# A decoder block on one core: head outputs turned in two fp32r parts, and the down products spread out between the turns

## The reference

```python
x = x + attn(layernorm(x))              # q, k, v; scores through a banded factor; softmax
x = x + xattn(layernorm(x), ctx, ctx)   # 8 heads of 32, exponential gates
x = x + ffn(layernorm(x))               # 256 -> 1024 -> 256, GELU, low-rank terms from the tokens
```

```python
maxit  = max(abs(sum(C, -1)), exp(-max_d))
H      = einsum('ij,jd->id', C, v) / (maxit + 1e-6)
xn     = (H - mean(H, over the 32 of the head)) / sqrt(var(H) + 1e-5)
out    = xn * gn_w + gn_b
```

## Time and profile before

| | |
|---|---|
| median of 3 runs | 1803.0 us |
| the profiled execution | 1803.04 us |
| its span from first to last instruction | 1801.3 us |
| mean granted TensorE clock, share of full | 0.984 |
| TensorE, products | 1742.0 us busy, 97% |
| TensorE, weight loads | 1376.2 us, 76% |
| VectorE | 1420.7 us, 79% |
| ScalarE | 1172.1 us, 65% |
| GpSimd | 402.0 us, 22% |
| mean DMA rate | 52 GB/s |

### The profile page before, as it was taken

How to read it: one execution, slowest core, us unless ns; L and a number is a source line. 1 busy time by engine, 2 the same in 40 slices (tenths; PEclk the granted TensorE clock), 3 DMA queues, 4 the chain that set the end, 5 groups by cost and what they waited for, 6 DMA issues and landing times.

```text
span 1801.3 us, 47658 instructions
## 1 busy us (share of the span) xinstructions
PE 1742.0 (97%) x15708; PEld 1376.2 (76%) x15708; DVE 1420.7 (79%) x4092; ACT 1172.1 (65%) x2666; POOL 402.0 (22%) x330
## 2 busy tenths in 40 slices
PE   5689999999999999999999999999999999999897
PEld 5568777777877777787777887777778777878676
DVE  6777888887888888788788888888888888887752
ACT  2556767666677766676766667776666676666552
POOL 1222122222122222212222212222221222222120
PEclk9789999999999999999999999999999999999998
DMA  5122121222112122212122211212221121221000
GB/s 142 37 51 57 30 61 40 61 62 61 50 36 62 38 62 62 60 32 54 49 51 62 61 52 34 62 38 62 62 61 40 47 59 41 62 62 44 24 13 27
DMA packets 226879, 93.05 MB, mean 52 GB/s; under 512 B 154896, under 2 KB 226320, under 8 KB 226848
## 3 DMA queue, kind: packets, MB, share of 16 engines
q1 hardware_dynamic: 226848, 92.65, 19.9%
HBM read 70.84 MB, written 16.78 MB: 49 GB/s over the span
## 4 chain that ended last, share of the span: by engine, by line
PE 94%; DVE 3%; ACT 1%; issue 1%; DMA 0%; SPq 0%; DVEq 0%; ACTq 0%
PE UA L1509 12%; PE TA L1509 6%; PE GT L1509 6%; PE UB L1440 6%; PE TB L1440 6%; PE PV L1440 5%; PE GT L1521 3%; PE UA L1465 3%; PE QQ L1267 3%; PE TA L1403 3%; PE TA L1440 3%; PE UA L1440 3%; PE DD L1267 2%; PE PV L1562 2%; PE UB L1562 2%; PE QQ L1547 2%
## 5 line engine op out<-in xcount | busy, mean ns | idle before, releaser
L1136 DVE TENSOR_TENSOR C<-qT,QKs 128x512 f32<-128x512 f32 x256 | 176.5, 709 | 126.6 <-ACT qT L785 123.5
L1509 PE MATMUL UA<-W2f,hs_all 128*128 128x256 f32 x1024 | 236.3, 379 | 0.0
L1509 PEld LDWEIGHTS UA<-W2f,hs_all 128*128 128x128 f32 x1024 | 194.4, 190 | 30.5 <-issue 0.2
L594 POOL TENSOR_TENSOR ot<-xg,b_b 128x1024 f32<-128x1024 f32 x32 | 76.4, 2388 | 553.4 <-DMA out<-ot 500.1
L629 POOL TENSOR_TENSOR Ng<-HT,gnw_b 128x256 f32<-128x256 f32 x128 | 93.3, 729 | 441.8 <-DVE cden L1149 437.3
L623 POOL TENSOR_TENSOR xg<-x,gnb_b 128x1024 f32<-128x1024 f32 x32 | 75.5, 2361 | 282.9 <-DVE Evl L1128 274.9
L1509 PE MATMUL TA<-W2f,hs_all 128*128 128x256 f32 x512 | 125.9, 379 | 0.0
L1509 PE MATMUL GT<-W2f,hs_all 128*128 128x256 f32 x512 | 115.8, 379 | 0.0
L695 ACT ACTIVATE V<-QQ 128x260 f32<-128x260 f32 x32 | 12.4, 388 | 145.8 <-PE QQ L1297 135.4
L1509 PEld LDWEIGHTS GT<-W2f,hs_all 128*128 128x128 f32 x512 | 94.8, 190 | 11.7
L1509 PEld LDWEIGHTS TA<-W2f,hs_all 128*128 128x128 f32 x512 | 94.8, 190 | 11.1 <-issue 0.2
(11 more groups left out here) (389 smaller groups left out, 5383.6 us busy)
## 6 DMA issues: line engine op xcount, KB each, us to landing
xin<-x SPq DMA_DIRECT2D x32, 512.0 KB, 4.4
xb<-x SPq DMA_DIRECT2D x32, 512.0 KB, 4.1
blocks<-ctx SPq DMA_DIRECT2D x256, 64.0 KB, 2.0
vc<-ctx SPq DMA_DIRECT2D x32, 512.0 KB, 3.6
out<-ot SPq DMA_DIRECT2D x32, 512.0 KB, 3.2
Ev<-xn SPq DMA_DIRECT2D x256, 4.0 KB, 1.7
hs_all<-L_ffn_W SPq DMA_DIRECT2D x4, 512.0 KB, 8.7
E<-xn SPq DMA_DIRECT2D x128, 16.0 KB
```

The costliest lines, as they stand in the source:

```text
L594: pool.tensor_tensor(ot[:, :, :], x3[:, :, :], b2_b[:, :].unsqueeze(1).broadcast_to([P, G, D]), ALU.add).then_inc(xf_ok.h, 1)
L1136: dve.tensor_tensor(C[:, b % 2, :, half], dx[hf].rearrange("p (h i) -> p h i", h=HEADS), QKs[:, b, :, half], ALU.mult)\
L1509: ins = pe.matmul(OB[b][:, 0:D], hs_all[:, k, b * S:(b + 1) * S], W2f[:, k, :], start=(i == 0), stop=(i == KH - 1))
```

## The change

Three of the four head outputs (b = 0, 1, 2) are now kept as two fp32r parts: ScalarE writes the high part `HSh` straight from PSUM, VectorE subtracts it from the same PSUM bank and writes the rest `HSl` (`head_low`), and `turn_h` multiplies each part with `centre_r`, an fp32r copy of `centre`, adding both in PSUM. The fourth (b = 3) stays as it was. In VectorE's list `head_low(b)` stands between the two `weigh_qk` of sequence b + 1. In TensorE's list the eight products of `down(1)`, before in runs of 2, 2 and 4 behind the turns, are divided in runs of 2, 1, 2, 1 and 2, three of which stand ahead of the turns.

```diff
-        HS = sb("HS", [P, 2, D])
+        HS = sb("HS", [P, D])
+        HSh, HSl = (sb(n, [P, 2, D], F32R) for n in ("HSh", "HSl"))
+        centre_r = sb("centre_r", [P, P + 4], F32R)
...
-                    act.activation(HS[:, b % 2, :], PB[b % 2][:, 0:D], ACT.Copy).then_inc(HS_ok.h, 1)
+                    act.activation(HSh[:, b % 2, :] if b < G - 1 else HS[:, :], PB[b % 2][:, 0:D], ACT.Copy).then_inc(HS_ok.h, 1)
...
+            done(dve.tensor_copy(centre_r[:, :], centre[:, :]))
...
+                def head_low(b):
+                    dve.wait_ge(HS_ok.h, HS_ok.at(it, b + 1))
+                    dve.wait_ge(ht_mm.h, ht_mm.at(it, max(b - 1, 0)))
+                    dve.tensor_tensor(HSl[:, b % 2, :], PB[b % 2][:, 0:D], HSh[:, b % 2, :].bitcast(F32), ALU.subtract)\
+                       .then_inc(HSl_ok.h, 1)
...
                     weigh_qk(1, 0)
+                    head_low(0)
                     weigh_qk(1, 1)
...
                     head_sums(0)
                     weigh_qk(2, 0)
+                    head_low(1)
                     weigh_qk(2, 1)
...
                     weigh_qk(3, 0)
+                    head_low(2)
                     weigh_qk(3, 1)
...
                 def turn_h(b):
-                    pe.wait_ge(HS_ok.h, HS_ok.at(it, b + 1))
+                    if b == G - 1:
+                        pe.wait_ge(HS_ok.h, HS_ok.at(it, G))
+                        parts, weights = (HS,), centre
+                    else:
+                        pe.wait_ge(HSl_ok.h, HSl_ok.at(it, b + 1))
+                        parts, weights = (HSh[:, b % 2, :], HSl[:, b % 2, :]), centre_r
                     for k in range(2):
-                        ins = pe.matmul(PB[b % 2][:, k * (P + 4):(k + 1) * (P + 4)], HS[:, b % 2, k * P:(k + 1) * P],
-                                        centre[:, :], start=True, stop=True)
+                        for i, part in enumerate(parts):
+                            ins = pe.matmul(PB[b % 2][:, k * (P + 4):(k + 1) * (P + 4)], part[:, k * P:(k + 1) * P],
+                                            weights[:, :], start=(i == 0), stop=(i == len(parts) - 1))
...
                 if own:
                     turn_probs()
+                if ffn:
+                    down(1, range(0, 2))
                 if cross:
                     turn_h(0)
                     decay(2, 0)
-                if ffn:
-                    down(1, range(0, 2))
-                if cross:
                     pv(1)
                     decay(2, 1)
                 if own:
                     attend(0)
                     attend(1)
+                if ffn:
+                    down(1, range(2, 3))
                 if cross:
                     turn_h(1)
                     decay(3, 0)
                 if ffn:
-                    down(1, range(2, 4))
+                    down(1, range(3, 5))
                 if cross:
                     pv(2)
                     decay(3, 1)
                 if own:
                     attend(2)
                     attend(3)
+                if ffn:
+                    down(1, range(5, 6))
                 if cross:
                     turn_h(2)
                 if ffn:
-                    down(1, range(4, KH))
+                    down(1, range(6, KH))
                     adapt(0)
```

More of the change, by code:

```diff
@@ L372, in build @@
         HT_ok = per_step("HT_ok", CROSS, G)
+        HSl_ok = per_step("HSl_ok", CROSS, G - 1)
         sq_ok = per_step("sq_ok", CROSS, G)
@@ L1664 @@
 V_MASKS = V_BIAS + 1 + 1 + 3 + 3 + 3 + 2
-SETUP_V = V_MASKS + 2 + 4 + 4 + 2
+SETUP_V = V_MASKS + 2 + 4 + 4 + 1 + 2
 def kernel(**inputs):
```

## The result

The changed kernel takes 1827.65 us (median of 4 runs, 1825.6 to 1828.5) against 1803.5 us beside it: a ratio of 1.0135, with a 95% interval of 1.0123 to 1.0148. It is slower. The profiled execution has a span of 1826.8 us, 25.5 us more than before, at the same granted clock of 0.984.

The account below looks back on a forecast made before the run. TensorE's list was taken to bound the kernel: 0.54 + 0.35 - 0.04 = 0.85 us a step, 25.5 us over 30 full steps, plus 2 at the ends, on 1803.0 gives 1830 us; own range 1820 to 1838, wider 1806 to 1845.

Parts of the forecast that it names:

- TensorE's list sets the step, and a wait is lost in full: TensorE is busy all step, so work removed is won and waits are lost in full, unless another engine binds.
- The window of 52.8 us: Steady-state window read as a whole step of the kernel before, with TensorE busy for all of it.
- the bounds of the two waits: Per step, attend(0) on PT loses 0.45 to 0.65 us, turn_h(1) on its low part 0.15 to 0.5.
- turn_h(0) covered, its price on ScalarE: First turn starts without a wait but 0.87 us later; PT_copy follows late on ScalarE, so attend(0) loses 0.54 us.
- turn_h(1) 0.35 us late: Second output: one down product of 0.43 us is too little cover, and TensorE waits 0.35 us for head_low(1).
- turn_h(2) without a wait: Third output: 1.5 us of TensorE work covers some 1.0 us of hs(2) and head_low(2), unless weigh_qk(3,0) is late.
- The turns: Three two-part turns a step: weight loads set the pace, 0.44 to 0.46 us each, gain at most 0.02 each.
- The ends: The two end steps with cross attention: partly covered subtractions cost about 1 us in each, 2 us together.
- (a): Rival: turns do get faster, 0.24 us, but waits stay; net +0.23 us a step, 1810 us; chance 0.14.
- (b): Rival: faster than before, turns of 0.24 us save 0.66 us a step, 1783 to 1799 us; chance 0.11.
- (c): Rival: loads and products one after the other, a turn of 0.65 us, 1847 us; chance 0.11.
- (d): Rival: no change, down products cover the waits by chance and turns cost the same; chance 0.04.

Follow-up runs that it names:

- The moves alone: The kernel before with only TensorE's new order, all turns fp32 and no subtraction on VectorE: 1820.9 us.
- PT_copy first: The changed kernel with PT_copy ahead of ht(0) on ScalarE instead of behind it: 1814.2 us.
- the new runs: The changed kernel with PT_copy ahead of ht(0) and the down products in runs of 2, 2, 1, 1, 2: 1803.45 us.
- the kernel of the high part twice: The kernel before, in its own order, with the first three turns as fp32r products of the high part taken twice, no subtraction: 1798.5 us.
- In bf16: The kernel before, in its own order, with the first three turns as bf16 products of the high part taken twice, no low part: 1780.2 us.

## Why the prediction was right

Forecast 1830 us, measured 1827.65, and the mechanism held step by step. That the number is so near is in part luck: the waits cost 0.97 us a step (53.93 - 52.95 = 0.98 against the kernel with as many fp32r products and no subtraction), where 0.89 was forecast, and the turns gave back 0.15 where 0.04 was taken.

*TensorE's list sets the step, and a wait is lost in full.* Held: 0.83 us a step in the trace, 0.85 in the sum. Two figures were loose. The window of 52.8 us is not one whole step, which takes 53.10; the sum did not use it. And the bounds of the two waits with the 2 us of the ends give 1823 to 1839.5, not 1820 to 1838.

*turn_h(0) covered, its price on ScalarE.* Held. The first turn and pv(1) show no wait. PT_copy starts 2.64 us after the transposes, where the working has 996.44 - 993.73 = 2.71. attend(0) starts 3.35 us after them instead of 2.87, 0.48 later; forecast 0.54, with a turn of the old length, and the turn ahead of it is 0.05 shorter. The late group then takes 0.96 us instead of 0.86. The forecast put that 0.1 into the start of attend(0), and it comes behind it; the start itself is 1011.53 - 1011.40 = 0.13 after PT all the same. So the whole wait costs 0.62, low by 0.08 in the forecast and inside its bounds of 0.45 to 0.65. The moves alone give the wait without any two-part turn, and PT_copy first takes it away: that is shown, not argued.

*turn_h(1) 0.35 us late.* Held, in place and in size: TensorE is through its down product at 1012.49 + 0.43 = 1012.92, and the turn's 0.40 us ends at 1013.67, so it starts in effect at 1013.27, 0.35 late. With the first wait gone and one more product ahead of the turn, the step loses another 0.37 us.

*turn_h(2) without a wait.* Held: in the lists of waits, bank PV (turns 0 and 2) has 2.1 us in four waits in the changed kernel.

*The turns.* Right in mechanism as far as the runs can tell, low in size: at most 0.02 us was taken off a turn, 0.05 was measured, and a step gained 0.15 instead of the 0.04 of the sum. The loads start 0.11 us apart. The Trainium skill has it in "TensorE: Matmul & The Clock Gate", section "LDWEIGHTS (loading the stationary operand)": columns over 1.2 GHz, 107 ns here. By that rule, the trace agrees at 0.11 us between loads and 0.106 us a pair.
*The ends.* 2 us forecast; between the profiled executions half a microsecond is left for the steps that aren't full, between the medians nothing. At step 2 the changed kernel is 155.43 - 153.42 = 2.0 us behind, but that says little of the change: the same product stands at 152.44 with PT_copy first and at 153.56 with the new runs too. Why was not looked into.

*The rivals.* (a) and (b), turns at half the price, fell with the kernel of the high part twice, a turn of 0.40 us. In bf16 the price of (a) is real: 0.23 us a turn. The pair took 0.106 to 0.114 us in fp32r and 57.5 ns in bf16. The Trainium skill, "TensorE: Matmul & The Clock Gate", section "Back-to-back issue gap", has N / 2.4 + 2.5 ns for an isolated product, an estimate of 57.5 ns for 132 columns. By that rule, the trace agrees with bf16 weights and disagrees where each product loads 128 columns of fp32r weights. (c), loads and products in a row, would have taken 0.165 us a pair and fell with the same figure. (d) fell with the result.

What stays open: the fp32r kernel with both waits covered takes 5 us more than the one with the high part twice and no subtraction. Of that, 53.08 - 52.95 = 0.13 us a step, 4 us in 30 steps, lies in the full steps. Turns 1 and 2 take 0.45 us there from the group ahead to the group behind, instead of 0.40, with a wait of 0.18 on their first load, most of it behind running products; that is 0.10. The rest was not located.

## What to carry to other kernels

When one engine has no gaps, cost a reordering on the others first: write down each instruction that stands behind the moved one in every list, and compare the delay with the smallest slack of those that wait for it; here 0.87 us was asked of a copy that had 0.45. A product with its own 128 columns of fp32r weights and few columns to stream is priced by the weight load, as far as these runs show, so splitting fp32 in two fp32r parts buys next to nothing at 132 columns (0.106 to 0.114 us a pair, where 260 columns take 0.12); bf16 parts do, if the values allow it. Read a group's price over both of its boundaries. And before you cover a wait, find it in the list of waits: the one of pv(1) was not there, and that of `xn3h` was.

## What the hardware showed that was not expected

An fp32r product of 66 columns costs as much as one of 132 when each has its own weights (1797.45 and 1798.5 us for 384 pairs of a kernel). The same pair in bf16 takes 0.0575 us at 132 columns, against 0.106 in fp32r (six pairs of a full step left out). An fp32 record of 132 columns with its load takes 0.115, little more than the fp32r one, but that need not be the load: at the 0.215 us of its 256-column records, 132 columns of fp32 would take an estimate of 0.11 for the columns alone. So the two agree at 132 columns, and the runs don't show that they do at fewer.
